# Cross-attention with a state-space tail on one Trainium2 core: the score maxima are turned by VectorE instead of TensorE, grouped in pairs in the context stage, and the last V projection gets another PSUM bank

## The chip, the cores and the metric

The kernel runs on one core of a Trainium2 chip. The metric is the device time of one execution in microseconds (us). Engine names in rows are PE (TensorE, matmuls), PEld (TensorE's weight loads), DVE (VectorE), ACT (ScalarE), POOL (GpSimd) and SPq (the DMA queue of SyncE). PSUM has eight banks of 512 fp32 words per partition; TensorE writes them, VectorE and ScalarE read them.

## The reference, cut to what matters

```python
x = layernorm(builder_state, g1, beta1)            # 4096 x 512
base_n = layernorm(base_state, g1, beta1)          # 3202 x 512, the context
q, k, v = heads(x, Wq, bq), heads(base_n, Wk, bk), heads(base_n, Wv, bv)     # 8 heads of 64
scores = einsum('bhqd,bhkd->bhqk', q, k) / sqrt(64)
out = softmax(scores) @ v ; x = residual + out @ W_o.T + b_o
U = (layernorm(x, g2, beta2) @ W_in.T + b_in) @ Bmat
s = silu(s @ A.T) + u_t                            # a scan over 4096 tokens
result = x + s @ Cmat + program_probs.mean(1) @ W_prog.T + b_prog
```

The change touches only how the softmax obtains, for each query, the number that is subtracted from its scores: their maximum over the keys (taken over scores of reduced precision).

## The kernel before

**Stages.** Token groups of 256 rows are normalised, turned by TensorE (`turn`), and projected: 16 groups `n` of queries, then 13 context groups (`g` = 0 to 12, `n` = 16 + `g`) to keys (`project_k`, four chunks of heads) and values (`project_v`, two tiles). Then comes the attention: 32 units `u`, each of one block of 512 queries and one pair of heads; a unit has 13 steps `j` of two key tiles. Then come the output projection, the second norm, the scan and the output. All engines have their programs written out by hand; semaphores alone tie them. What stands below is in the order of the code.

**Maxima.** Before unit `w` runs, its maxima must be known. For each of 26 numbers `m`, `maxima(w, m)` makes one pair of matmuls (one per head, each on 64 rows of the array): queries of one quarter (`m % 4`) as the stationary operand against 512 keys (`m // 4`); the last two, `m` = 24 and 25, take the 130 keys left over. `take_max(w, m)` on VectorE reduces the pair to a column of `mx_part`. Unit `u` has two of them in every step for the unit after it, so that `m` = 24, 25 of unit `u + 1` stand in step 8 of unit `u`. 34 of them are done early, in the context stage (`ctx_maxima`): in groups 2 to 11 two of unit 0, and from group 3 on most often a third of another; in group 12 the last five.

**From maxima to shift.** `row_max(w)` (L1016) reduces `mx_part` to `mx_row` (128 partitions, 8 columns). `turn_max(w)` (L1364) turns it on TensorE to 8 rows of 128, ScalarE's `shift(w)` (L725) copies it with its sign changed to `shift_row`, and SyncE's `send_shift(w)` writes it to memory and reads it back as `sh[w % 2]`; `spread_shift` also loads it to all partitions as `shb`. Two ways use it: `shift_scores` on TensorE adds `ones_row` times `sh` to the scores of a tile, and for the odd tiles of units after the first VectorE adds `shb` in `add_shift` (L1094). ScalarE then takes the exponential (L799). In step 9 (`TURN_STEP`) of a unit stand `turn_max(u + 1)` on TensorE and `shift(u + 1)` on ScalarE.

**Banks.** In the context stage `turn` writes banks 0 and 1, K chunks use 2 to 4, `project_v` 7, and the early maxima 5 and 6, one pair after another. In the attention scores use banks 0 to 3, maxima 4 and 5, the P times V product 6, and 7 is shared by `turn_max` and the sums over keys (`spread_sum`, step 3).

**GpSimd** adds up exponentials in `accp` (L605) and issues DMAs that add others in `acca` and `accb`; the sum of a unit ends in `acca` (L636) and is read in step 3 of the next.

## Time and profile before

| what | us |
|---|---|
| runs shown | 2253.38, 2254.17, 2255.58; median 2254.17 |
| profiled execution | 2255.61, its span 2253.8 |
| TensorE busy | 2216.3 (98%) |
| VectorE busy | 1713.4 (76%) |
| GpSimd busy | 1584.2 (70%) |
| ScalarE busy | 1092.4 (48%) |

The span runs from the first to the last instruction of the profile; 1.8 us lie around it. The queries' projections end at about 133 us, the context stage at 316 us, the attention at about 2080 us. A row of a timeline gives the start, the duration, engine, line, operation, tiles, shapes and count, and in brackets the idle time of the engine before it with what ended it. A busy PE is one whose pipeline holds a matmul; the distance between the starts of two groups of matmuls says better what a group costs.

### The profile page before, as it was taken

The page shows a single profiled execution, that of the slowest core. Times are in us where ns is not written, and L with a number is a line of the kernel's source. Part 1 is how long each engine was busy: PE and PEld are TensorE (multiplying, and loading weights), DVE is VectorE, ACT ScalarE, POOL GpSimd, SP SyncE. Part 2 cuts the span into 40 slices and gives each one's busy share as a digit, 9 for nine tenths or more (in the row PEclk, how much of TensorE's full clock was granted, in tenths as well). Part 3 has the DMA queues.
Part 4 walks back from the last instruction along what each step waited for, and adds up shares of the span by engine and source line. Part 5 has one row for each costly group of instructions (what it writes and reads, how often), then busy time and mean ns, then how long its engine had stood idle before and what let it go on. Part 6 is the DMA issues. An engine that isn't in the chain of part 4 may idle for free.

```text
span 2253.8 us, 36015 instructions
## 1 busy us (share of the span) xinstructions
PE 2216.3 (98%) x14120; PEld 1279.2 (57%) x14120; DVE 1713.4 (76%) x2087; ACT 1092.4 (48%) x1418; POOL 1584.2 (70%) x1038
## 2 busy tenths in 40 slices
PE   8999999999999999999999999999999999999997
PEld 8998865555555555555555555555555555445774
DVE  7866546888888888888888888888888888763776
ACT  5654334444454444444544544444445444453454
POOL 1200027888888888888888888888888888889332
PEclk9999999999999999999999999999999999999999
DMA  7750226777777777777777777777777777787844
GB/s 273 233 162 10 75 85 139 156 157 160 156 159 160 159 170 168 171 170 167 168 161 160 167 170 171 171 171 164 163 163 165 167 166 166 160 182 159 265 149 150
DMA packets 170091, 365.45 MB, mean 162 GB/s; under 512 B 28537, under 2 KB 75001, under 8 KB 169410
## 3 DMA queue, kind: packets, MB, share of 16 engines
q0 software_dynamic: 59904, 218.13, 47.4%
q1 hardware_dynamic: 110018, 145.02, 20.3%
q8 instruction: 112, 1.84, 0.3%
q14 instruction: 57, 0.47, 0.1%
HBM read 95.82 MB, written 49.04 MB: 64 GB/s over the span
## 4 chain that ended last, share of the span: by engine, by line
PE 94%; DMA 1%; ACT 1%; DVE 1%; issue 1%; POOL 1%; SPq 0%; DVEq 0%; ACTq 0%; POOLq 0%
PE ps L1478 34%; PE ps L1343 11%; PE ps L1455 8%; PE ps L1457 8%; PE ps L1459 8%; PE ps L1447 5%; PE ps L1306 4%; PE ps L1314 3%; PE ps L1324 3%; PE ps L1545 3%; PE ps L1278 1%; DMA acca<-pt 1%; PE ps L1348 1%; PE ps L1488 1%; PE ps L1608 1%
## 5 line engine op out<-in xcount | busy, mean ns | idle before, releaser
L799 ACT ACTIVATE pt<-ps 128x1024 f32<-128x1024 f32 x800 | 777.6, 1021 | 891.8 <-PE ps L1459 882.0
L1005 DVE TENSOR_REDUCE mx_part<-ps 128x2 f32<-128x1024 f32 x768 | 938.1, 1221 | 339.5 <-PE ps L1343 339.5
L605 POOL TENSOR_TENSOR accp<-accp,pt 128x1024 f32<-128x1024 f32 x416 | 1032.9, 2483 | 210.0 <-ACT pt L799 204.7
L1478 PE MATMUL ps<-pt,v 128*64 128x512 f32 x3328 | 805.6, 605 | 0.0
L1094 DVE TENSOR_TENSOR ps<-ps,shb 128x1024 f32<-128x1024 f32 x403 | 493.2, 1224 | 46.7 <-PE ps L1459 46.7
L1478 PEld LDWEIGHTS ps<-pt,v 128*64 128x64 f32 x3328 | 201.8, 136 | 345.2 <-issue 339.0
L1343 PE MATMUL ps<-kk,qh 64*128 64x512 f32 x1520 | 344.4, 448 | 1.6 <-DVE mx_part L1005 1.6
L1343 PEld LDWEIGHTS ps<-kk,qh 64*128 64x128 f32 x1520 | 141.6, 183 | 340.9 <-DVE mx_part L1005 250.0
L1455 PE MATMUL ps<-qh,kk 64*128 64x512 f32 x1664 | 328.9, 390 | 2.7 <-ACT pt L799 2.7
L1457 PE MATMUL ps<-qh,kk 64*128 64x512 f32 x1664 | 329.3, 390 | 0.0
L1459 PE MATMUL ps<-ql,kk 64*128 64x512 f32 x1664 | 328.5, 389 | 0.0
L615 POOL DMA_DIRECT2D acca<-pt x192 | 179.0, 932 | 5.0 <-DMA acca<-pt 3.9
L1455 PEld LDWEIGHTS ps<-qh,kk 64*128 64x128 f32 x1664 | 157.2, 184 | 37.7 <-ACT pt L799 4.1
L1457 PEld LDWEIGHTS ps<-qh,kk 64*128 64x128 f32 x1664 | 157.6, 184 | 34.8
L1459 PEld LDWEIGHTS ps<-ql,kk 64*128 64x128 f32 x1664 | 157.9, 184 | 34.1
L1447 PE MATMUL ps<-sh,ones_row 64*128 64x512 f32 x858 | 173.2, 400 | 1.2 <-ACT pt L799 1.2
L594 POOL MEMSET sh<- 128x512 f32 x2 | 1.0, 530 | 190.3 <-PE ps L1324 190.3
L625 POOL DMA_DIRECT2D accb<-pt x128 | 124.9, 976 | 0.2 <-POOL accp L605 0.2
L1545 PE MATMUL ps<-wo_hl,og 128*128 128x512 f32 x384 | 93.0, 396 | 0.5 <-DVE x_last L1137 0.4
L1447 PEld LDWEIGHTS ps<-sh,ones_row 64*128 64x128 f32 x858 | 82.1, 186 | 15.2 <-ACT pt L799 11.8
L1545 PEld LDWEIGHTS ps<-wo_hl,og 128*128 128x128 f32 x384 | 70.5, 188 | 19.6 <-issue 5.7
L631 POOL TENSOR_TENSOR accp<-accp,accb 128x1024 f32<-128x1024 f32 x32 | 76.9, 2403 | 4.6
(165 smaller groups left out, 1779.7 us busy)
## 6 DMA issues: line engine op xcount, KB each, us to landing
acca<-pt POOLq DMA_DIRECT2D x224, 512.0 KB, 4.9
accb<-pt POOLq DMA_DIRECT2D x160, 512.0 KB, 4.8
q_scratch<-kk SPq DMA_DIRECT2D x32, 512.0 KB, 4.3
acca<-accp POOLq DMA_DIRECT2D x32, 512.0 KB, 4.6
o_scratch<-ost SPq DMA_DIRECT2D x32, 512.0 KB, 3.1
og<-o_scratch SPq DMA_DIRECT2D x32, 512.0 KB, 6.2
shb<-m_scratch SPq DMA_DIRECT2D x31, 512.0 KB, 4.6
xs<-x SPq DMA_DIRECT2D x16, 512.0 KB, 6.5
```

The costliest lines, as they stand in the source:

```text
L605: nc.gpsimd.tensor_tensor(acc[:, :], acc[:, :], pt[n % PT_SLOTS][:, :], ALU.add).then_inc(added_p, 1)
L615: nc.gpsimd.dma_start(acc[:, :], pt[n % PT_SLOTS][:, :], accum_op=ALU.add).then_inc(added_a[u % 2], 16)
L799: nc.scalar.activation(pt[n % PT_SLOTS][:, :], src, ACT.Exp, scale=SCALE).then_inc(exped, 1)
L1005: nc.vector.tensor_reduce(mx_part[w % 2][:, m % QT, :, m // QT], ps[:, b:b + 2, :], AX_X, ALU.max)\
L1094: nc.vector.tensor_tensor(ps[:, b:b + 2, :], ps[:, b:b + 2, :], shb[u % 2][:, :, :], ALU.add)\
L1343: ins = mm(ps[:, bank, :], q[r, (m % QT) * P:(m % QT + 1) * P], kk[r, p, 0, a:a + QB], start=True, stop=True)
L1447: ins = mm(ps[:, 2 * (t % 2) + h, :], ones_row[r, :], sh[u % 2][r, :], start=first, stop=not first)
L1455: mm(ps[:, b + h, :], kk[r, p, 0, key], qh[u % 3][r, :], start=first, stop=False)
L1457: mm(ps[:, b + h, :], kk[r, p, 1, key], qh[u % 3][r, :], start=False, stop=False)
L1459: ins = mm(ps[:, b + h, :], kk[r, p, 0, key], ql[u % 2][r, :], start=False, stop=last)
L1478: ins = mm(ps[HD * h:HD * (h + 1), 6, :], v[:, t, f:f + HD], pt[n % PT_SLOTS][:, h * QB:(h + 1) * QB], start=(t == 0), stop=(t == NT - 1))
L1545: ins = mm(ps[:, 2 + t, :], og[:, d % OG_SLOTS, a, k, rows], wo_hl[:, b, k], start=(i == 0), stop=(i == len(PASSES) - 1))
```

## The change

Four things change together.

1. **Turning.** `turn_max` and `shift` are gone, with their semaphores. `mx_row` is now 32 columns wide (24 of them cleared once), VectorE turns it in blocks of 32 by 32 into `mx_turn`, directly behind the reduction, and `send_shift` stores it with four DMAs of 8 rows by 32 words instead of one of 8 by 128. The sign is no longer changed: `ones_row` holds -1 and `add_shift` subtracts.
2. **Pairing.** In context groups 2 to 11 the second early maximum follows the first directly, ahead of the second V tile, in banks 0 and 1, once those have been read by the norm's copies. VectorE takes it after the second K chunk's low part.
3. **The last V tile** of the context goes to bank 6 (`v_bank`) when all early maxima are taken, so it does not wait for the copy of the tile before it.
4. **`spread_sum`** no longer waits for the shift.

```diff
+def v_bank(n, t):
+    return 6 if n == NG - 1 and t == 1 else 7
+def second_max(g):
+    return (0, 2 * (g - 2) + 1) if 2 <= g < C_G - 1 else None
 def max_bank(w, m):
+    if w == 0 and m % 2 == 1 and m < 2 * (C_G - 3):
+        return 0
     return 5 if (w, m) in EARLY else 4
...
             def send_shift(w):
-                sp.wait_ge(shift_ready, w + 1)
+                sp.wait_ge(max_ready, w + 1)
...
-                sp.dma_start(m_scratch[w % 2].rearrange("h (q k) -> (h q) k", k=P), shift_row[:, :].bitcast(F32)).then_inc(sh_stored, 16)
-                sp.wait_ge(sh_stored, 16 * (w + 1))
+                by_tile = m_scratch[w % 2].rearrange("h (q k) -> (h q) k", k=P)
+                for i in range(4):
+                    sp.dma_start(by_tile[:, 32 * i:32 * (i + 1)], mx_turn[32 * i:32 * i + 2 * QT, :].bitcast(F32)).then_inc(sh_stored, 16)
+                sp.wait_ge(sh_stored, 64 * (w + 1))
...
-            def shift(w):
-                act.wait_ge(max_turned, w + 1)
-                wait(act, sh_stored, 16 * w)
-                nc.scalar.activation(shift_row[:, :], ps[0:2 * QT, turn_bank(w), 0:P], ACT.Copy, scale=-1.0)\
-                    .then_inc(shift_ready, 1)
...
             def row_max(w):
...
-                wait(dve, max_turned, w)
-                nc.vector.tensor_reduce(mx_row[:, :, :].rearrange("p h q -> p q h"), mx_part[w % 2][:, :, :, :], AX_X, ALU.max)\
-                    .then_inc(max_ready, 1)
+                nc.vector.tensor_reduce(mx_row[:, 0:2 * QT].rearrange("p (h q) -> p q h", h=2), mx_part[w % 2][:, :, :, :], AX_X, ALU.max)\
+                    .then_inc(row_ready, 1)
+                dve.wait_ge(row_ready, w + 1)
+                wait(dve, sh_stored, 64 * w)
+                nc.vector.transpose(mx_turn[:, :].bitcast(F32), mx_row[:, :].bitcast(F32)).then_inc(max_ready, 1)
...
             def turn(n):
                 pe.wait_ge(normed, n + 1)
                 wait(pe, n_ready, 2 * n)
+                if second_max(n - 2 - X_G):
+                    pe.wait_ge(max_taken, nth_max(*second_max(n - 2 - X_G)) + 1)
...
             def project_v(n, t):
                 g = n - X_G
-                wait(pe, v_ready, GT * g + t)
+                if v_bank(n, t) == 7:
+                    wait(pe, v_ready, GT * g + t)
+                else:
+                    pe.wait_ge(max_taken, M_EARLY)
...
-                wait(pe, max_taken, nth_max(w, m))
+                if max_bank(w, m) == 0:
+                    wait(pe, max_taken, nth_max(w, m) - 1)
+                    pe.wait_ge(n_ready, 2 * (X_G + m // 2 + 2 + 2))
+                else:
+                    wait(pe, max_taken, nth_max(w, m))
...
             project_v(NG - 1, 0)
-            turn_max(0)
             project_v(NG - 1, 1)
             pe.wait_ge(k_ready, FC * C_G)
-            pe.wait_ge(shift_ready, 1)
+            pe.wait_ge(max_taken, M_EARLY)
...
-                    if ahead and j == TURN_STEP:
-                        turn_max(u + 1)
```

On TensorE, in a context group with three maxima, the order before is this (x11 is the rest of 12 matmuls; `qh` marks a maximum of unit 0, `qx` one of unit 1; L1314 is V, L1324 a K chunk, L1343 a maximum, L1278 the turning of the next group).

```order
L1343 MATMUL ps<-kk,qh_64 128x512 [waits max_taken,k_ready]
L1343 MATMUL ps<-kk,qh_64 128x512
L1314 MATMUL ps<-wkv,n_63 128x512 [waits v_ready]
L1314 MATMUL ps<-wkv,n_63 128x512 x11
L1343 MATMUL ps<-kk,qh_64 128x512 [waits max_taken,k_ready]
L1343 MATMUL ps<-kk,qh_64 128x512
L1324 MATMUL ps<-n_63,wkv 128x256 [waits k_ready]
L1324 MATMUL ps<-n_63,wkv 128x256 x11
L1324 MATMUL ps<-n_63,wkv 128x256 [waits k_ready]
L1324 MATMUL ps<-n_63,wkv 128x256 x11
L1343 MATMUL ps<-kk,qx 128x512 [waits max_taken,k_ready]
L1343 MATMUL ps<-kk,qx 128x512
```

In the changed kernel, where V is L1321, K L1331 and a maximum L1354, the same place reads so.

```order
L1354 MATMUL ps<-kk,qh_64 128x512 [waits max_taken,k_ready]
L1354 MATMUL ps<-kk,qh_64 128x512
L1354 MATMUL ps<-kk,qh_64 128x512 [waits n_ready,max_taken,k_ready]
L1354 MATMUL ps<-kk,qh_64 128x512
L1321 MATMUL ps<-wkv,n_63 128x512 [waits v_ready]
L1321 MATMUL ps<-wkv,n_63 128x512 x11
L1331 MATMUL ps<-n_63,wkv 128x256 [waits k_ready]
L1331 MATMUL ps<-n_63,wkv 128x256 x11
L1331 MATMUL ps<-n_63,wkv 128x256 [waits k_ready]
L1331 MATMUL ps<-n_63,wkv 128x256 x11
L1354 MATMUL ps<-kk,qx 128x512 [waits max_taken,k_ready]
L1354 MATMUL ps<-kk,qx 128x512
```

The second pair of maxima has moved ahead of the V tile and stands beside the first, with one wait more.

In step 9 of a unit of the attention, TensorE has this before, from the end of the scores (L1459) over the second maximum (L1343) to P times V (L1478).

```order
L1455 MATMUL ps<-qh_65,kk 128x512 x2
L1457 MATMUL ps<-qh_65,kk 128x512 x2
L1459 MATMUL ps<-ql_68,kk 128x512 x2
L1364 MATMUL ps<-ident,mx_row 8x128 [waits den_taken,max_ready]
L1343 MATMUL ps<-kk,qh_64 128x512 [waits max_taken]
L1343 MATMUL ps<-kk,qh_64 128x512
L1478 MATMUL ps<-pt_71,v 64x512 [waits exped]
L1478 MATMUL ps<-pt_71,v 64x512
```

And this in the changed kernel.

```order
L1455 MATMUL ps<-qh_65,kk 128x512 x2
L1457 MATMUL ps<-qh_65,kk 128x512 x2
L1459 MATMUL ps<-ql_68,kk 128x512 x2
L1354 MATMUL ps<-kk,qh_64 128x512 [waits max_taken]
L1354 MATMUL ps<-kk,qh_64 128x512
L1478 MATMUL ps<-pt_71,v 64x512 [waits exped]
L1478 MATMUL ps<-pt_71,v 64x512
```

The turning of the row maxima is gone, and the maximum follows the scores, all of them on 64 rows of the array.

At the end of the context stage TensorE has this before, from the last early maxima over the two V tiles to the first maximum of the attention.

```order
L1348 MATMUL ps<-kk,qh_64 128x130 [waits max_taken,k_ready]
L1348 MATMUL ps<-kk,qh_64 128x130 x3
L1314 MATMUL ps<-wkv,n_63 128x512 [waits v_ready]
L1314 MATMUL ps<-wkv,n_63 128x512 x11
L1364 MATMUL ps<-ident,mx_row 8x128 [waits n_ready,max_ready]
L1314 MATMUL ps<-wkv,n_63 128x512 [waits v_ready]
L1314 MATMUL ps<-wkv,n_63 128x512 x11
L1343 MATMUL ps<-kk,qh_65 128x512 [waits max_taken,ones_set,qh_loaded_1,shift_ready,k_ready]
```

And this in the changed kernel.

```order
L1359 MATMUL ps<-kk,qh_64 128x130 [waits max_taken,k_ready]
L1359 MATMUL ps<-kk,qh_64 128x130 x3
L1321 MATMUL ps<-wkv,n_63 128x512 [waits v_ready]
L1321 MATMUL ps<-wkv,n_63 128x512 x11
L1321 MATMUL ps<-wkv,n_63 128x512 [waits max_taken]
L1321 MATMUL ps<-wkv,n_63 128x512 x11
L1354 MATMUL ps<-kk,qh_65 128x512 [waits max_taken,ones_set,qh_loaded_1,k_ready]
```

The turning between the V tiles is gone, and the second V tile waits for maxima taken instead of the copy of the first tile.

## Rows read from the trace of the kernel before

**Rows 1.** The page, part 1: busy us, share of the span, instructions
```profile
PE 2216.3 (98%) x14120; PEld 1279.2 (57%) x14120; DVE 1713.4 (76%) x2087; ACT 1092.4 (48%) x1418; POOL 1584.2 (70%) x1038
```

**Rows 2.** TensorE in steps 7 to 10 of a unit: start, duration (us)
```profile
1005.28 0.50 PE L1343 MATMUL ps<-kk,qh 64*128 64x512 f32 x2
...
1005.62 0.39 PE L1447 MATMUL ps<-sh,ones_row 64*128 64x512 f32 x2
...
1007.23 0.39 PE L1343 MATMUL ps<-kk,qh 64*128 64x512 f32 x2
...
1007.55 1.94 PE L1478 MATMUL ps<-pt,v 128*64 128x512 f32 x8
...
1009.42 0.44 PE L1348 MATMUL ps<-kk,qh 64*128 64x130 f32 x4
...
1013.50 0.50 PE L1343 MATMUL ps<-kk,qh 64*128 64x512 f32 x2
...
1015.53 0.08 PEld L1364 LDWEIGHTS ps<-ident,mx_row 128*8 128x8 f32 x1 [0.35 <-issue]
...
1018.04 0.50 PE L1343 MATMUL ps<-kk,qh 64*128 64x512 f32 x2
```

**Rows 3.** Line L1364: duration ns min/median/max, first and last start us
```profile
L1364 PE MATMUL ps<-ident,mx_row x32: 272/273/274, 311.9 to 2003.1; 128*8 128x128 f32 x32
```

**Rows 4.** Timeline of VectorE and GpSimd at the row maximum (L1016) of that unit
```profile
1012.69 2.37 POOL L605 TENSOR_TENSOR accp<-accp,pt 128x1024 f32<-128x1024 f32 x1 [0.94 <-ACT pt L799]
...
1012.75 0.21 DVE L1016 TENSOR_REDUCE mx_row<-mx_part 128x8 f32<-128x56 f32 x1
...
1014.11 1.23 DVE L1005 TENSOR_REDUCE mx_part<-ps 128x2 f32<-128x1024 f32 x1 [1.15 <-PE ps L1343]
```

**Rows 5.** Timeline of TensorE, a context group without maxima
```profile
146.04 2.99 PE L1314 MATMUL ps<-wkv,kk 128*128 128x512 f32 x12
...
148.87 3.04 PE L1324 MATMUL ps<-kk,wkv 128*128 128x256 f32 x24
```

**Rows 6.** Timeline of TensorE, context group 6
```profile
216.25 3.03 PE L1324 MATMUL ps<-n,wkv 128*128 128x256 f32 x24
219.21 0.49 PE L1343 MATMUL ps<-kk,qh 64*128 64x512 f32 x2
219.64 3.06 PE L1314 MATMUL ps<-wkv,n 128*128 128x512 f32 x12
222.62 0.50 PE L1343 MATMUL ps<-kk,qh 64*128 64x512 f32 x2
223.06 3.12 PE L1324 MATMUL ps<-n,wkv 128*128 128x256 f32 x24
226.11 0.49 PE L1343 MATMUL ps<-kk,qx 64*128 64x512 f32 x2
226.53 1.09 PE L1278 MATMUL ps<-ident,xs 128*128 128x128 f32 x8
```

**Rows 7.** Timeline at the end of the context: PEld, ACT, SPq
```profile
307.45 4.18 PEld L1314 LDWEIGHTS ps<-wkv,n 128*128 128x128 f32 x12
...
311.68 0.08 PEld L1364 LDWEIGHTS ps<-ident,mx_row 128*8 128x8 f32 x1
...
312.39 0.57 ACT L714 ACTIVATE v<-ps 128x512 f32<-128x512 f32 x1
...
312.56 0.30 SPq L413 DMA_DIRECT2D m_scratch<-shift_row  x1
...
313.01 2.61 PEld L1314 LDWEIGHTS ps<-wkv,n 128*128 128x128 f32 x12 [1.25 <-ACT v L714]
...
313.79 0.57 SPq L415 DMA_DIRECT2D sh<-m_scratch  x1
```

**Rows 8.** Windows: busy us by engine (PE, PEld, DVE, ACT, POOL), PEclk, DMA
```profile
307.00:312.00 5.00, 4.92 (x17) 3.73 (x17) 0.92 (x2) 0.00 (x0) 0.00 (x0) 0.66 0.70 243
```

**Rows 9.** Timeline: the latest sum over the keys in the loop
```profile
1923.91 0.16 PEld L1488 LDWEIGHTS ps<-acca,ones 128*32 128x32 f32 x8 [0.89 <-DMA acca<-accp]
```

More of the change, by code:

```diff
@@ L55, in maxima_of @@
     return [(i // NM, i % NM) for i in range(first, min(first + 2, NM * UNITS))]
-TURN_STEP = NJ - M_LEAD
 PAIR_ORDER = [2, 3, 0, 1]
@@ L770, in _ @@
                 high_k(C_G - 1, i)
-            shift(0)
             for t in range(GT):
@@ L825, in _ @@
                         high_o(u - 1)
-                    if j == TURN_STEP and u + 1 < UNITS:
-                        shift(u + 1)
                     if u == UNITS - 2 and j in (3, 5, 7, 9):
@@ L1000, in take_max @@
                 if m == 0:
-                    wait(dve, max_ready, w - 1)
+                    wait(dve, row_ready, w - 1)
                 dve.wait_ge(max_done, nth_max(w, m) + 1)
@@ L1071, in _ @@
                     if g < C_G - 1:
+                        low_k(g, 0)
                         for w, m in early[:1]:
                             take_max(w, m)
-                        for i in (0, 1):
-                            low_k(g, i)
+                        low_k(g, 1)
                         for w, m in early[1:2]:
@@ L1356, in early_maxima @@
                     maxima(w, m)
-            def turn_max(w):
-                pe.wait_ge(max_ready, w + 1)
-                wait(pe, den_taken, w - 1)
-                if w == 0:
-                    pe.wait_ge(n_ready, 2 * NG)
-                nc.tensor.transpose(ps[0:2 * QT, turn_bank(w), 0:P], mx_row[:, :, :].rearrange("p h q -> p (h q)"), ident[:, :])\
-                    .then_inc(max_turned, 1)
             pe.wait_ge(consts, 2)
@@ L1484, in spread_sum @@
                 pe.wait_ge(added_a[u % 2], 16 * (len(A_TILES) + 1) * (u // 2 + 1))
-                if u + 1 < UNITS:
-                    pe.wait_ge(shift_ready, u + 2)
+                wait(pe, den_taken, u)
                 for i in range(4):
```

24 lines of the change are left out of this document (12 added, 12 removed).

## The prediction

> **What bounds the kernel now.** I read the page's shares first, then the timeline of TensorE in the attention, where the kernel spends about 1760 of its 2254 us. TensorE is busy for 2216.3 of 2253.8 us; VectorE, next, has 76% and GpSimd 70% [rows 1]. So what leaves TensorE's queue is time won, as long as no other engine then ends last. In the timeline the reader should compare the distances between the first maxima of successive steps: step 7 takes 1009.42 - 1005.28 = 4.14 us, step 8, whose two maxima are the short ones of 130 keys, takes 4.08, and step 9, which alone holds the turning of the row maxima, takes 1018.04 - 1013.50 = 4.54 [rows 2]. Within a step a pair of 64-row matmuls that follows the first maximum starts 0.34 us after it (1005.62), and the product with V, on all 128 rows, starts 0.32 us behind the second maximum (1007.55 after 1007.23) [rows 2].
>
> **The change part by part.**
>
> Turning in the loop. TensorE loses L1364, one matmul of 0.27 us, 32 in all: 31 in the attention, one at the end of the context [rows 3]. Its price is not the 0.27 but what the step gets longer: the array leaves the 64-row scores (its weight load sat idle for 0.35 us), does the turning, and goes back to 64 rows for the second maximum, which now follows the scores directly. 4.54 - 4.14 = 0.40 us a unit, times 31 = 12.4 us. From below, the idle 0.35 alone gives 10.9; from above, 4.54 - 4.08 gives 14.3 [rows 2]. I take 12.4, since step 7 has the same matmuls as step 9 without its turning.
>
> What VectorE gets in return. It turns 128x32 words, an operation that the trace does not show, and waits for its own reduction before it. The nearest row is that reduction of 56 elements a partition, 0.21 us; the farthest, the reduction of 1024, takes 1.23 [rows 4]. 32 elements are nearer to the first: I take 0.2, with 0.1 for the wait. Queued behind it is the first maximum of step 9, and for that VectorE stands idle for 1.15 us, until TensorE has made it [rows 4]. So the turning is hidden, and costs nothing; at 1.23 plus the wait it would run over by 0.2 us, and this much VectorE would be late in step 9. The Trainium skill ("VectorE: DVE Perf Modes", section The three transpose paths) gives 311 ns for VectorE's turning of 128x128 bf16. An estimate by that page, about 0.3 us here, would leave the sum as it is; no run so far shows it.
>
> ScalarE loses 32 small copies; it is busy for 48% [rows 1] and nothing hangs on it. SyncE issues four stores of the shift instead of one, some 4 x 0.3 us by L413 [rows 7], but starts when VectorE is done in step 8, over 4 us ahead of the old start behind step 9. The loads `sh` and `shb` queued behind them come earlier, not later, and are first needed in step 0 of the next unit.
>
> Pairing in the context. In group 6 from the first maximum to the turning of the next group is 226.53 - 219.21 = 7.32 us: pair to V 0.43, V to pair 2.98, pair to K 0.44, K to pair 3.05, pair to turning 0.42 [rows 6]. Afterwards the order is pair, pair, V, K, K, pair: 0.34 for the first pair and 0.32 for the second, as steps of the loop show them [rows 2], V to K 2.83 as in a group without maxima [rows 5], K to pair 2.96 as it is behind an undisturbed V (216.25 to 219.21), and 0.42: 6.87 us. This saves 0.45 us in each of ten groups, 4.5 us. From below, with 0.43 instead of 0.32 and 3.05 instead of 2.96, it is 0.25, 2.5 us; from above, if the second pair takes no more than its 512 columns at 2.4 GHz, 0.21 instead of 0.32, it is 0.56, 5.6 us. The new waits cost nothing by the rows: between the turning that fills banks 0 and 1 and the pair that wants them stand a V tile and two K chunks, 2.83 + 2.96 = 5.8 us, as many as between the pair and the next turning, and VectorE has two reductions of 1.23 and a few smaller operations to do in each. The first pair uses banks 5 and 6, the second 0 and 1, so neither waits for the reduction of the other.
>
> End of the context. V's first tile loads its last weights until 307.45 + 4.18 = 311.63; then TensorE turns the row maxima at 311.68, ScalarE copies the shift and then the tile until 312.96, and the second tile starts at 313.01 [rows 7]. With its own bank, and all early maxima taken long before, it can start at about 311.65: 1.35 us. TensorE's clock belongs to this place: over 307 to 312 the granted clock is 0.66 on the mean [rows 8], which is 3.4 us at 1.2 instead of 2.4 GHz. If the lower level lasted into the second tile, twelve matmuls that load weights for 2.61 us could lose up to 2.6; at the other bound the clock is back as before. I take 1.35, from -1.2 to 1.4. The shift of unit 0 must then arrive earlier. It is ready on VectorE 3 us before the old copy, its four stores take some 1.2 us to issue, and the store's way to the next issue is 313.79 - 312.56 = 1.23 us [rows 7]; `sh` would be issued at about 311.5, 2.3 us sooner than now, where only 1.35 are asked for. Covered.
>
> Sum: 12.4 + 4.5 + 1.35 = 18.2 us. The profiled execution took 2255.61 with a span of 2253.8; it becomes 2235.6 in span and 2237.4 in time. It lies 1.4 above the median of the runs, 2254.17, which becomes 2236.0. By the lower bounds the sum is 10.9 + 2.5 - 1.2 = 12.2 (2242.0), by the upper ones 14.3 + 5.6 + 1.4 = 21.3 (2232.9).
>
> **The rivals.**
>
> *The sums over the keys become late* (chance 0.08). Each unit of the attention becomes 0.4 us shorter for GpSimd and its DMAs too. `spread_sum` in step 3 waits for the last DMA into `acca`, and in one unit TensorE's weight load stood for 0.89 us because of it [rows 9]. If GpSimd could not follow at all, the 12.4 us would be given back, and the time would be 2254.17 - 5.8 = 2248.3. For it speaks that one unit; against it GpSimd's 70% and that in the unit of rows 4 it sat idle for 0.94 us ahead of one addition, waiting for ScalarE.
>
> *Pairing gives nothing* (0.11). The two pairs wait for something between them, a bank or VectorE, or the V tile starts later by what the pair gained. Then 4.5 us are missing: 2240.5. Against it speaks that VectorE has 2.98 us between the two pairs now, and two reductions of 1.23 with a K chunk's low part between fit before the second K chunks are done.
>
> *Slower: VectorE's turning is held up by GpSimd* (0.05). In the unit read, GpSimd begins an addition at 1012.69 that lasts 2.37 us, to 1015.06, and VectorE would come to its turning at about 1013.0, behind its reduction [rows 4]. If the turning could not run beside it, VectorE would be free at about 1015.3 and its first maximum of step 9 start 1.2 us late. Each step hangs from VectorE's second maximum of the step before with hardly 0.1 us to spare (the first reduction begins 0.61 us into the step, and it, the addition of the shift, on as many elements, and the second reduction take about 1.2 us each, an estimate of 4.1 of the 4.14 us), so all 1.2 us would reach TensorE, 31 x 1.2 = 37 us: 2236 + 37 = 2273. It decides from 18.2 / 31 = 0.6 us of overrun in a unit on, that is from 1.75 us of turning with its waits. Against it: the reduction at 1012.75 ran in 0.21 us beside the same addition. The Trainium skill ("SBUF — State Buffer", section Who interferes with whom) says that VectorE's copies and `tensor_scalar` can enter modes that use a port pair shared with GpSimd, where the second to come is blocked for a whole instruction, and that reductions never do; of the turning it says nothing. The reduction's row agrees with the page. The page's rule, if it held for the turning, would be this rival.
>
> **How the numbers follow.** The forecast that the sum holds gets the remaining 0.76. A measurement of this kernel can tell about 0.2%, 4.5 us, from no change. The time predicted is the forecast's, 2236. Its own bounds, 2232.9 to 2242.0, hold the second rival's 2240.5 too; with the run-to-run scatter of about 1 us this gives 2232 to 2243, which leaves out the first and the third rival, 0.13, and a little of the tails. Faster by over 0.2%: the forecast, the second rival and most of the first, 0.93; within 0.2%: 0.02; slower: 0.05.
>
> **What would show it.** In the profile after: step 9 of a unit takes 4.14 us, and units follow each other 0.4 us closer; the turning on VectorE takes 0.1 to 0.3 us and the idle time before its next maximum is shorter by as much and still above 0; a context group with three maxima takes 0.45 us less; the second V tile of the last group starts within 0.1 us of the first one's last weights. The prediction is wrong if steps 8 or 9 get longer on VectorE, if `spread_sum` waits for `acca` in many units, or if the clock falls in places where it stood at its upper level before.

## The result, and the profile after

The changed kernel takes 2241.92 us (median of five runs, 2239.28 to 2242.49), the kernel before 2254.17 (five runs). The ratio is 0.9941, with a 95% interval of 0.9928 to 0.9954: faster by 12.25 us, and by the interval 10.4 to 16.2, where the sum said 18.2. The profiled execution took 2239.28 us with a span of 2237.5, so the two profiled executions lie 16.3 us apart. The missing 6 us thus have two parts: 1.9 us that the profiled pair lacks of the sum, and 4.1 us by which the medians lie closer together than the profiled pair (the profiled execution of before lies 1.4 above its median, that of after 2.6 below its own). The second part is hardly more than the interval of the ratio allows.

The page of the changed kernel, part 1, answers to [rows 1]: TensorE lost 15.9 us of busy time and 32 instructions, VectorE gained 5.1 us and 33 instructions.

```profile
PE 2200.4 (98%) x14088; PEld 1275.1 (57%) x14088; DVE 1718.5 (77%) x2120; ACT 1088.5 (49%) x1386; POOL 1586.4 (71%) x1038
```

The timeline of TensorE in step 9 and the step behind it (a maximum is now L1354), to be read against [rows 2]:

```profile
786.89 0.50 PE L1354 MATMUL ps<-kk,qh 64*128 64x512 f32 x2
...
788.61 0.39 PE L1459 MATMUL ps<-ql,kk 64*128 64x512 f32 x2
788.83 0.44 PE L1354 MATMUL ps<-kk,qh 64*128 64x512 f32 x2
789.20 1.94 PE L1478 MATMUL ps<-pt,v 128*64 128x512 f32 x8
791.07 0.50 PE L1354 MATMUL ps<-kk,qh 64*128 64x512 f32 x2
...
795.21 0.50 PE L1354 MATMUL ps<-kk,qh 64*128 64x512 f32 x2
```

The second maximum follows the scores after 0.22 us. Step 9 takes 791.07 - 786.89 = 4.18 us, the next 4.14. Over the 30 units between the first and the last short maxima of the attention, step 9 is 4.19 on the mean where it was 4.56: 0.37 a unit, not 0.40. The missing 0.04 is between the second maximum and the product with V (0.37 us in step 9, 0.32 in [rows 2]). The units as a whole follow each other 0.42 us closer (54.89 to 54.47). Half of what goes beyond step 9 is one pause: TensorE of the kernel before waits 1.09 us at 1926.30, behind the place of [rows 9], for ScalarE, which waits for a DMA into `acca`; the changed kernel has 0.30 us there. The weight load of [rows 9] itself says little: it sits idle for 0.81 us in the 30 other units too, and in 30 units of the changed kernel.

VectorE at the row maximum, against [rows 4]:

```profile
1003.90 0.21 DVE L1014 TENSOR_REDUCE mx_row<-mx_part 128x8 fp32r<-128x56 f32 x1
1004.15 0.21 DVE L1018 STREAM_TRANSPOSE mx_turn<-mx_row 128x32 f32<-128x32 f32 x1
1005.25 1.23 DVE L1002 TENSOR_REDUCE mx_part<-ps 128x2 f32<-128x1024 f32 x1 [0.89 <-PE ps L1354]
```

The turning takes 0.21 us, starts 0.25 us behind the start of the reduction, and leaves 0.89 us of idle time ahead of the next maximum. It took 0.21 us all 32 times, and 31 of the 32 lay wholly inside an addition of GpSimd.

TensorE in context group 6, against [rows 6]:

```profile
215.89 3.03 PE L1331 MATMUL ps<-n,wkv 128*128 128x256 f32 x24
218.85 0.73 PE L1354 MATMUL ps<-kk,qh 64*128 64x512 f32 x4
219.51 3.06 PE L1321 MATMUL ps<-wkv,n 128*128 128x512 f32 x12
222.41 3.03 PE L1331 MATMUL ps<-n,wkv 128*128 128x256 f32 x24
225.37 0.49 PE L1354 MATMUL ps<-kk,qx 64*128 64x512 f32 x2
225.79 0.87 PE L1282 MATMUL ps<-ident,xs 128*128 128x128 f32 x6
```

Both pairs are one group of four, 0.66 us long, and nothing in it waits. From the first maximum to the next turning is 6.94 us where it was 7.32: 0.38 instead of the 0.45 of the sum, because V to K takes 2.90 and not 2.83.

The end of the context, the first maximum of the attention before, then TensorE and SyncE's queue of the changed kernel, against [rows 7]:

```profile
315.97 0.50 PE L1343 MATMUL ps<-kk,qh 64*128 64x512 f32 x2
```

```profile
304.49 0.44 PE L1359 MATMUL ps<-kk,qh 64*128 64x130 f32 x4 [1.08 <-DVE mx_part L1006]
304.86 7.36 PE L1321 MATMUL ps<-wkv,n 128*128 128x512 f32 x24
312.15 0.50 PE L1354 MATMUL ps<-kk,qh 64*128 64x512 f32 x2
```

```profile
306.31 1.31 SPq L419 DMA_DIRECT2D m_scratch<-mx_turn  x4
309.94 0.57 SPq L421 DMA_DIRECT2D sh<-m_scratch  x1
```

The two V tiles are one group now. The first maximum of the attention starts at 312.15, 3.82 us earlier than before (315.97), the first V tile 2.59 us earlier: the place itself gave 1.23. `sh` is issued 2.2 us ahead of the attention's first maximum and 3.85 us earlier than before, of which 2.59 are the earlier stage; the 1.26 that are left are less than the prediction's 2.3, but TensorE has no wait for `sh` at the start of the attention.

**Where the profiled pair lost 1.9 us of the sum.** I followed the same marks through both traces. At the last maximum (L1359, for unit 31) the changed kernel is 16.4 us ahead, where the sum, with 30 of its 31 steps 9, has 17.9. Of this 1.4 us, 0.7 are the pairing's, 0.1 the end of the context's, and 1.1 lie ahead of the first early maximum, which starts at 165.07 us instead of 163.95; the loop gave 0.6 more than its term. At the first output projection the lead is 15.0; at the end 16.3. What comes back at the end goes with the clock: in the output stages the granted clock is 0.53, 0.50, 0.50 and 0.76 over 2226 to 2234 us before, and 0.97, 0.50 and 0.68 over 2208 to 2214 after, which is 3.4 and 1.7 us of the upper level's time. The stretch that gives time back is the last unit, 1.4 us, or 1.8 with the 31st turning that it has no more. There TensorE, ScalarE and GpSimd wait for DMAs. The rows are of the changed kernel, for SyncE, GpSimd, ScalarE and TensorE in this order:

```profile
1999.79 2.61 SPq L499 DMA_DIRECT2D og<-o_scratch  x4
...
2011.54 0.89 POOL L642 DMA_DIRECT2D acca<-accp  x1 [3.89 <-DMA acca<-pt]
...
2019.45 1.02 ACT L798 ACTIVATE pt<-ps 128x1024 f32<-128x1024 f32 x1 [3.64 <-DMA acca<-pt]
...
2020.53 0.50 PE L1455 MATMUL ps<-qh,kk 64*128 64x512 f32 x2 [2.67 <-ACT pt L798]
```

And of the kernel before, GpSimd, ScalarE and TensorE at the same place of the program:

```profile
2028.39 0.89 POOL L636 DMA_DIRECT2D acca<-accp  x1 [4.03 <-DMA acca<-pt]
...
2034.48 1.02 ACT L799 ACTIVATE pt<-ps 128x1024 f32<-128x1024 f32 x1 [1.80 <-DMA acca<-pt]
...
2035.56 0.50 PE L1455 MATMUL ps<-qh,kk 64*128 64x512 f32 x2 [1.08 <-ACT pt L799]
```

SyncE loads the attention's outputs for the first projection (`og`, 2 MB in four DMAs) while the last accumulating DMAs of unit 30 are under way. The accumulating DMA beside them takes 9.6 us to land before and 9.8 after, and GpSimd's next one is issued after a wait of 4.03 and 3.89 us. TensorE's wait at 2035.56 (before) and 2020.53 (after) grew from 1.08 to 2.67 us. From the last maximum to the first projection is 74.7 us before and 76.1 after.

**The longer wait comes from a later DMA.** The activation that TensorE waits for at 2020.53 waits for the accumulating DMA issued at 2013.10, when all four loads of `og` have landed (the last at 2012.3). This DMA takes 6.2 us. The profile's view of the DMAs has it, and while it is under way, from 2015.9 to 2016.5 us, a packet of another queue:

```profile
acca<-pt POOLq DMA_DIRECT2D x1, 512.0 KB, 6.2
...
q8 instruction: 1, 0.02, 9.3%
```

The second line is a packet of 16 KB of the queue that the profile calls instruction. The same DMA in `step9_same`, which is the changed kernel with one matmul more in step 9 (below), and TensorE behind it:

```profile
acca<-pt POOLq DMA_DIRECT2D x1, 512.0 KB, 4.4
...
2021.51 0.50 PE L1455 MATMUL ps<-qh,kk 64*128 64x512 f32 x2 [1.09 <-ACT pt L798]
```

Eleven profiles of this case have the loads of `og` at their old place. In five of them (the changed kernel, `after_again`, `turn_only`, `dve_4`, `dve_8`) such a packet starts 33.1 to 33.6 us behind the last maximum, while this DMA is under way; the DMA takes 6.10 to 6.25 us, TensorE waits 2.66 to 2.76, and the stretch takes 76.1 to 78.8. In the other six (before, `pair_only`, `bank_only` and the three of `step9`) the packet comes outside of it; the DMA takes 4.4 us, TensorE waits 1.08 to 1.10, and the stretch takes 74.1 to 75.0. The five have no matmul at the place of the turning in step 9, the six have one. So the longer wait goes with the change, but by where the packet falls, and not because the last unit stops what TensorE won upstream: `step9_same` has the turning on VectorE and takes 74.8. That the packet delays the DMA is an inference from this coincidence; no run moved the packet alone.

### The profile page after: what moved, and what is told of

The parts are those of the page before. It is cut to its first block, busy times and chain, and to the rows that moved or that the text cites. A ratio compares the mean times of both kernels' runs of the same rounds, so it can differ in the third digit from the quotient of the medians.

```text
span 2237.5 us, 35987 instructions
## 1 busy us (share of the span) xinstructions
PE 2200.4 (98%) x14088; PEld 1275.1 (57%) x14088; DVE 1718.5 (77%) x2120; ACT 1088.5 (49%) x1386; POOL 1586.4 (71%) x1038
## 4 chain that ended last, share of the span: by engine, by line
PE 93%; DMA 2%; issue 1%; ACT 1%; POOL 1%; DVE 1%; SPq 0%; DVEq 0%; ACTq 0%; POOLq 0%
PE ps L1478 33%; PE ps L1354 11%; PE ps L1455 8%; PE ps L1457 8%; PE ps L1459 8%; PE ps L1447 4%; PE ps L1310 4%; PE ps L1542 4%; PE ps L1321 3%; PE ps L1331 3%; DMA acca<-pt 1%; PE ps L1282 1%; POOL accp L611 1%; PE ps L1359 1%; PE ps L1487 1%
## 5 line engine op out<-in xcount | busy, mean ns | idle before, releaser
L611 POOL TENSOR_TENSOR accp<-accp,pt 128x1024 f32<-128x1024 f32 x416 | 1044.1, 2510 | 193.1 <-ACT pt L798 191.8
L1478 PE MATMUL ps<-pt,v 128*64 128x512 f32 x3328 | 805.6, 605 | 0.0
L1478 PEld LDWEIGHTS ps<-pt,v 128*64 128x64 f32 x3328 | 201.8, 136 | 344.6 <-issue 338.2
L1354 PE MATMUL ps<-kk,qh 64*128 64x512 f32 x1520 | 339.2, 444 | 1.7 <-DVE mx_part L1002 1.6
L1354 PEld LDWEIGHTS ps<-kk,qh 64*128 64x128 f32 x1520 | 140.9, 183 | 340.5 <-DVE mx_part L1002 257.7
L1459 PE MATMUL ps<-ql,kk 64*128 64x512 f32 x1664 | 328.1, 389 | 0.0
L621 POOL DMA_DIRECT2D acca<-pt x192 | 189.6, 987 | 5.4 <-DMA acca<-pt 4.0
L1459 PEld LDWEIGHTS ps<-ql,kk 64*128 64x128 f32 x1664 | 157.3, 184 | 34.4
L1447 PEld LDWEIGHTS ps<-sh,ones_row 64*128 64x128 f32 x858 | 82.1, 186 | 15.0 <-ACT pt L798 12.4
```

Source lines behind the costliest of these rows:

```text
L611: nc.gpsimd.tensor_tensor(acc[:, :], acc[:, :], pt[n % PT_SLOTS][:, :], ALU.add).then_inc(added_p, 1)
L621: nc.gpsimd.dma_start(acc[:, :], pt[n % PT_SLOTS][:, :], accum_op=ALU.add).then_inc(added_a[u % 2], 16)
L1354: ins = mm(ps[:, bank, :], q[r, (m % QT) * P:(m % QT + 1) * P], kk[r, p, 0, a:a + QB], start=True, stop=True)
L1447: ins = mm(ps[:, 2 * (t % 2) + h, :], ones_row[r, :], sh[u % 2][r, :], start=first, stop=not first)
L1459: ins = mm(ps[:, b + h, :], kk[r, p, 0, key], ql[u % 2][r, :], start=False, stop=last)
L1478: ins = mm(ps[HD * h:HD * (h + 1), 6, :], v[:, t, f:f + HD], pt[n % PT_SLOTS][:, h * QB:(h + 1) * QB], start=(t == 0), stop=(t == NT - 1))
```

## The experiments

What was open: whether each part of the change is worth what its rows say, where the rest of the 18.2 us went, and whether the price of 0.40 us for a matmul of 8 columns is that of the array's shape. Medians of "before" are those of the runs timed beside them on the same chip.

### The parts alone

`turn_only` is the changed kernel without pairing and without the bank; `pair_only` and `bank_only` are the kernel before with one part each; `after_again` is the changed kernel once more, timed beside them.

```diff
 # turn_only, on the changed kernel
-    return 6 if n == NG - 1 and t == 1 else 7
+    return 7
...
-    return (0, 2 * (g - 2) + 1) if 2 <= g < C_G - 1 else None
+    return None
...
-                        early_maxima(early[:2])
+                        early_maxima(early[:1])
                         project_v(n, 1)
+                        early_maxima(early[1:2])
...
 # pair_only, on the kernel before: the same lines the other way round, with max_bank's
+    if w == 0 and m % 2 == 1 and m < 2 * (C_G - 3):
+        return 0
...
 # bank_only, on the kernel before
-                wait(pe, v_ready, GT * g + t)
+                if v_bank(n, t) == 7:
+                    wait(pe, v_ready, GT * g + t)
+                else:
+                    pe.wait_ge(max_taken, M_EARLY)
...
```

> The kernel before with the first part of the change alone: the row maxima are turned by VectorE, and stored by four DMAs; early maxima and V banks as before. Theory A (the gain is the sum of what TensorE's queue loses, as the timelines show it): the units follow each other 0.39 us closer, 31 x 0.39 = 12.1 us, and the second V tile of the last context group still waits for ScalarE's copy, so about 12 to 12.5 us in all, ratio 0.9946. Theory B (the whole change gained 12.3 to 13.3 us in timed runs where its own timeline shows 16.3 because something in the loop gives time back that no single profile shows): well below 12 us, 8 or so.

> The kernel before with the second part alone: in context groups 2 to 11 the second early maximum stands beside the first, in banks 0 and 1. Theory A: ten groups of 13.58 instead of 13.96 us, 3.8 us, ratio 0.9983. Theory B (the pairing's gain is given back elsewhere, for example in a lower granted clock at the end of the context): about 1 us or nothing.

> The kernel before with the third part alone: the last V tile goes to bank 6 and does not wait for ScalarE's copy of the tile before it; the turning on TensorE still stands between the two. Theory A: the tile starts at about 312.0 instead of 313.0, 1.0 us. Theory B: the time at the lower clock gets longer by what was won, no gain.

> The changed kernel once more, so that it and its parts are timed on the same chip against the same runs of before. Theory A: the gain is the sum of the three parts run beside it, 16 us or so by the timelines. Theory B: less than the sum, 12 to 13 us as measured before.

| kernel | us (runs' lowest to highest) | ratio, 95% interval | below before (2253.63) |
|---|---|---|---|
| turn_only | 2244.12 (2243.26 to 2247.25) | 0.9961 (0.9947 to 0.9974) | 9.5 |
| pair_only | 2250.11 (2247.88 to 2253.69) | 0.9984 (0.9975 to 0.9993) | 3.5 |
| bank_only | 2251.75 (2250.10 to 2255.31) | 0.9995 (0.9986 to 1.0004) | 1.9 |
| after_again | 2241.68 (2241.37 to 2242.66) | 0.9948 (0.9934 to 0.9961) | 12.0 |

The order of the parts is that of the sum. Turning and pairing show by themselves; the bank's 1.9 us can't be told from nothing. The profiles give each part more sharply. In `turn_only` units follow each other 0.39 us closer, as expected, 11.7 us over 30 units. In `pair_only` the way from the first early maximum to the attention is 3.8 us shorter, as expected (148.26 instead of 152.02). In `bank_only` the two V tiles with the turning take 1.1 us less (7.39 instead of 8.52). The three medians add up to 14.9 us where all together give 12.0; an interval of a single ratio is some 3 us to each side for the short series, so this difference is not established.

The profile of `after_again` tells something that the first profile didn't: the clock. The rows are windows of 2 us in the last unit (span of the window, busy time of PE, PEld, DVE, ACT, POOL, granted clock, DMA share, GB/s), of the changed kernel's first profile and then of `after_again`:

```profile
2018.00:2020.00 2.00, 0.00 (x0) 0.00 (x0) 0.00 (x0) 0.55 (x1) 1.33 (x2) 1.00 0.40 162
2020.00:2022.00 2.00, 1.47 (x12) 1.05 (x12) 0.46 (x1) 0.48 (x1) 2.00 (x2) 1.00 0.35 68
```

```profile
2018.00:2020.00 2.00, 0.01 (x2) 0.00 (x0) 0.00 (x0) 0.40 (x1) 1.39 (x1) 0.90 0.48 193
2020.00:2022.00 2.00, 1.32 (x6) 1.13 (x8) 0.00 (x0) 0.62 (x1) 1.96 (x2) 0.50 0.34 68
2022.00:2024.00 2.00, 2.00 (x10) 0.97 (x10) 1.56 (x2) 0.35 (x1) 2.00 (x2) 0.50 1.03 197
2024.00:2026.00 2.00, 2.00 (x6) 0.47 (x4) 0.00 (x0) 1.86 (x3) 1.44 (x2) 0.50 0.69 131
2026.00:2028.00 2.00, 2.00 (x14) 1.01 (x12) 0.00 (x0) 0.00 (x0) 1.93 (x2) 0.89 0.74 132
```

In both TensorE stands still for the whole of 2018 to 2020. In the first profile the granted clock stays 1.00; in the second it falls to 0.50, the 1.2 GHz level, while the engine stands and stays there until 2026. The five windows lose 0.2 + 1 + 1 + 1 + 0.2 = 3.4 us of the upper level's time, and from the last maximum to the first projection takes 78.8 us instead of 76.1. `turn_only` shows the same (0.79, 0.50 and 0.86 from 2024 to 2030; 77.5 us), and so do `dve_4` (0.60 and 0.55 from 2020 to 2024; 77.4 us) and `dve_8` (0.74, 0.50 and 0.91 from 2048 to 2054; 77.4 us): 1.7 us each. The six profiles whose wait there is 1.1 us stay at 1.00. The mean clock of a run fits this: 3.4 us are 0.0015 of the span, and the first five runs of the changed kernel are 2239.28 and 2239.89 us at a mean clock of 0.998, and 2241.92, 2242.24 and 2242.49 at 0.996. That the slower three are the ones with this fall isn't shown. A mean over a whole run does not say where the clock fell, and it falls in two more places that differ between profiles: at the end of the context by 0 or 1.7 us of the upper level's time, in the output stages by 0, 1.7 or 3.4. Two of the runs of `after_again` took 2241.4 us at 0.998.

### The loads of the last unit moved

The loads of `og` are issued behind `spread_rden(u - 1)` of the last unit instead of ahead of it, when the accumulating DMAs have landed: `og_late_before` on the kernel before, `og_late_after` on the changed one.

```diff
                     sp.wait_ge(shifted, tiles_added(UNITS - 1))
-                    for d in (0, 1):
-                        load_og(d)
...
                     spread_rden(u - 1)
+                if u == UNITS - 1:
+                    for d in (0, 1):
+                        load_og(d)
```

> The kernel before, with the first four loads of the output projection's operand (og, 2 MB) issued behind the inverse sums of unit 30 instead of at the start of the last unit. Theory A (those loads collide with the last DMAs into acca of unit 30, whose landing then takes about 10 instead of 5 us, and ScalarE and TensorE wait): the last unit gets 2 to 4 us shorter, ratio 0.9985. Theory B (GpSimd's additions bound the last unit anyway, and the loads only happen beside): no change, or slower if the loads are then missed by the projection.

> The changed kernel with the same later loads. Theory A (the change wins 16 us up to the last unit, and loses 1.4 to 4 of them where these loads stand, by a longer pause of TensorE and the lower clock behind it): the pause of 2.7 us goes, the granted clock stays at its upper level there, and the kernel gains 4 to 6 us on the changed one; against the kernel before with late loads it is 15 to 16 us faster. Theory B (the missing 4 us of the timed runs are lost elsewhere): as much as the kernel before gains from late loads, so 12 to 13 us apart again.

In the traces the collision is gone from both: the accumulating DMA that took 9.6 and 9.8 us to land takes 5.1 and 4.9, the last maximum to the first projection takes 71.9 us (before: 74.7) and 72.1 us (after: 76.1), and in `og_late_after` TensorE has no pause at all in the stretch where it stood for 2.67 us. So the collision is shown to cost 2.8 us there in the kernel before, as theory A said; it is older than the change. The changed kernel's 4.0 us are not the collision's alone, since the later DMA takes 5.0 us in `og_late_after` instead of 6.2. In `og_late_alt` (below), whose loads are late too, it takes 6.5 us with an instruction packet beside it, TensorE waits 1.30 us at that place, and the stretch takes 73.6.

Late loads also cost something: in the first output projections TensorE now waits 2.19 us (`og_late_before`), 0.89 (`og_late_after`) and 2.00 (`og_late_alt`) for VectorE's `x_first`, where no profile with early loads has more than 0.41. Of the lead of 3.4 us that `og_late_after` has over the changed kernel at the first projection, 2.6 are left at the last one and 1.5 at the end (span 2236.0 against 2237.5), where its granted clock also lost 3.4 instead of 1.7 us.

In the timed runs the kernel before goes from 2254.55 to 2252.63 us (0.9992, 0.9983 to 1.0001), which can't be told from nothing, and the changed one stands at 2240.29 (0.9937, 0.9923 to 0.9950), 1.4 to 1.6 us below the earlier runs of the changed kernel. With late loads the two medians are 12.3 us apart, as theory B said and not 15 to 16. So it is not shown that the 4 us missing in the timed runs are lost at these loads; the intervals are too wide to exclude it.

`og_late_alt` adds to `og_late_after` that the odd early maxima of the last context group use banks 0 and 1 as well, so that TensorE doesn't wait for VectorE there.

```diff
-    if w == 0 and m % 2 == 1 and m < 2 * (C_G - 3):
+    if w == 0 and m % 2 == 1:
         return 0
...
-                    pe.wait_ge(n_ready, 2 * (X_G + m // 2 + 2 + 2))
+                    pe.wait_ge(n_ready, 2 * min(X_G + m // 2 + 2 + 2, NG))
```

> The changed kernel with late loads and, in the last context group too, odd early maxima of unit 0 in banks 0 and 1, so that none of the five waits for the reduction of the one before. Theory A (the pauses of 0.25, 0.25 and 1.1 us there go, and with the last one the 3.4 us at the lower clock behind it): 1.6 us from the pauses and up to 1.7 more from the clock, about 3 us faster than the kernel with late loads alone. Theory B (the clock falls there whatever these pauses are): 1 to 1.5 us.

It takes 2236.59 us (2233.24 to 2239.80), a ratio of 0.9915 (0.9902 to 0.9929) to the kernel before: the fastest median here, 17.96 us below before. It is 3.7 us below `og_late_after`, but the two intervals overlap (0.9923 to 0.9950), so the times alone don't choose between the theories. The end of its context stage, TensorE, and then the same of `dve_4`, whose context stage is the changed kernel's:

```profile
302.67 0.67 PE L1360 MATMUL ps<-kk,qh 64*128 64x130 f32 x8 [0.26 <-DVE mx_part L1003]
303.26 5.74 PE L1322 MATMUL ps<-wkv,n 128*128 128x512 f32 x24
308.93 0.50 PE L1355 MATMUL ps<-kk,qh 64*128 64x512 f32 x2
```

```profile
304.44 0.44 PE L1361 MATMUL ps<-kk,qh 64*128 64x130 f32 x4 [1.08 <-DVE mx_part L1006]
304.81 5.74 PE L1323 MATMUL ps<-wkv,n 128*128 128x512 f32 x24
310.47 0.50 PE L1356 MATMUL ps<-kk,qh 64*128 64x512 f32 x2
```

The pause of 1.08 us is gone: the last two groups of maxima are one. The pause of 0.26 ahead of them, and the one of 0.25 before it, are still there, so the expectation's list of what goes was too long. The two V tiles take 308.93 - 303.26 = 5.67 us instead of the changed kernel's 312.15 - 304.86 = 7.29. In the windows from 304 to 310 the granted clock is 1.00, where the changed kernel had 0.81, 0.50 and 0.84. But the clock is not shown to be the edit's doing: `dve_4` has the pause of 1.08 us, keeps 1.00 in the same windows, and takes 310.47 - 304.81 = 5.66; so does `step9_half`, with 5.65. Of the 13 profiles with this pause the clock stayed up in four (`dve_4`, `step9_half`, `turn_only`, `og_late_before`) and fell in nine. Against `dve_4`, at the same clock, the way from the first early maximum to the attention is 1.3 us shorter (144.14 against 145.44), which is theory B's size. The rest of the 3.7 us of the timed runs is not accounted for.

### What a matmul of another shape costs

Step 9 gets a matmul back whose result nobody reads, in the place where the turning stood. Each run has one of the three lines below; the flags `start` and `stop` are left out.

```diff
                         score_tile(u, 2 * j + 1)
+                    if ahead and j == 9:
+                        wait(pe, den_taken, u)
+                        mm(ps[0:8, 7, 0:P], ones[:, 0:8], ident[:, :])                   # step9_full
+                        mm(ps[0:8, 7, 0:P], ones[0:HD, 0:8], ident[0:HD, :])             # step9_half
+                        mm(ps[:, 7, 0:P], ones_row[0:HD, :], sh[u % 2][0:HD, 0:P])       # step9_same
                     for w, m in todo[1:]:
```

> The changed kernel with one matmul of constants put back where the turning stood in step 9 of every unit (128 rows, 8 columns of weights, 128 moving columns; its result is not used). Theory A (the price of the turning was that the array leaves the 64-row matmuls and comes back): step 9 takes 4.54 us again, 0.40 more. Theory B (the price was the turning's own waits for VectorE): 4.14 to 4.25 us.

> The same matmul on 64 rows only (its result is not used), so that it stands among 64-row matmuls. Theory A: what is left is its own 128 columns and issue, 0.05 to 0.1 us; step 9 takes about 4.2 us. If the price is the matmul's and not that of leaving the 64 rows: 4.5 us.

> The changed kernel with one matmul more in step 9 of each of 31 units, of 128 columns into bank 7, on 64 rows with 128 weight columns and fp32r operands: the array shape and type of the scores and maxima around it. It has 31 matmuls whose result is not read; the output does not depend on it. The 8-column matmuls cost 0.53 us a unit (4.67 and 4.66 us for step 9 instead of 4.14). Theory A2 (the price is that of a change of the array's shape, there and back): here nothing changes shape, so step 9 takes 4.14 + 0.05 to 0.15 = 4.2 to 4.3 us, and the one run lies 2 to 5 us above the changed kernel, 2241 to 2247. Theory B (any extra matmul with weights of its own between the scores and the second maximum costs about that much): step 9 takes 4.6 to 4.7 us, and the run 2250 to 2254.

TensorE in step 9 of one unit, from the added matmul or the scores ahead of it to the second maximum, first of `step9_full` (128 rows, 8 columns of weights), then of `step9_half` (64 rows, 8 columns), then of `step9_same` (64 rows, 128 columns, as all its neighbours):

```profile
791.96 0.39 PE L1459 MATMUL ps<-ql,kk 64*128 64x512 f32 x2
792.28 0.39 PE L1523 MATMUL ps<-ident,ones 128*8 128x128 f32 x2
792.60 0.50 PE L1354 MATMUL ps<-kk,qh 64*128 64x512 f32 x2
```

```profile
791.00 0.38 PE L1523 MATMUL ps<-ident,ones 64*8 64x128 f32 x2
791.31 0.50 PE L1354 MATMUL ps<-kk,qh 64*128 64x512 f32 x2
```

```profile
788.37 0.39 PE L1459 MATMUL ps<-ql,kk 64*128 64x512 f32 x2
788.60 0.22 PE L1523 MATMUL ps<-sh,ones_row 64*128 64x128 f32 x1
788.61 0.49 PE L1354 MATMUL ps<-kk,qh 64*128 64x512 f32 x2
```

Over 30 units step 9 takes 4.66, 4.66 and 4.26 us, against 4.19 without the matmul: the price is 0.47, 0.47 and 0.07. The runs give 2251.72, 2249.74 and 2240.68 us, one each. In the first two the small matmul starts 0.32 us behind the last scores, where scores follow each other after 0.23, and the next group 0.31 us behind it; in the third it starts 0.23 behind the last scores and the maximum at once behind it. `step9_same` fell where its expectation had the price of a change; the expectation for `step9_half` was wrong: leaving the rows of the array as they are doesn't avoid the price. So it is shown that the price isn't that of one more matmul, but of one that differs from its neighbours. All three wait for the same semaphore, so it isn't that wait either. The number of matmuls isn't it: the first two are two in the rows, the turning of the kernel before was one and cost 0.37.

In what it must differ, these three runs don't show: the first two, like the turning of the kernel before, have plain fp32 operands on 8 columns, the third has its neighbours' type (fp32r) and shape, so type and shape changed together. The ordinary step doesn't separate them either. A group of the same shape follows the scores after 0.22 or 0.23 us (788.61 to 788.83 in the changed kernel), the product with V after 0.32, and the second 64-row pair behind it starts 0.34 us after the first [rows 2]; but `v` and `pt` are plain fp32 and the scores are fp32r. The pairing separates them. In a context group the maxima (64 rows), the V tiles and the K chunks (128 rows) are all fp32r, and putting two pairs of maxima side by side takes away one change of shape and one change back, with the same matmuls (the second pair in other banks). That is worth 7.32 - 6.94 = 0.38 us, the size of the turning's 0.37. So a change of shape there and back costs about as much as the turning did with the type left alone; what a change of type costs alone wasn't tried.

### How much room VectorE has

`dve_4` and `dve_8` let VectorE turn the same block four and eight times more ahead of the one that counts.

```diff
                 wait(dve, sh_stored, 64 * w)
+                for _ in range(4):                 # dve_8: range(8)
+                    link(nc.vector.transpose(mx_turn[:, :].bitcast(F32), mx_row[:, :].bitcast(F32)))
                 nc.vector.transpose(mx_turn[:, :].bitcast(F32), mx_row[:, :].bitcast(F32)).then_inc(max_ready, 1)
```

> The changed kernel with four more turnings of the same row on VectorE before the one that counts, each waiting for the one before (about 0.25 us each, 1.0 in all). VectorE stands idle for 0.7 to 0.9 us before its next maximum now. Theory A (what goes beyond that idle time reaches TensorE): steps 9 get up to 0.2 us longer, 31 x 0.2 = 6 us at most. Theory B (VectorE has more room behind): no change.

> The same with eight more, about 2.0 us. Theory A: 1.1 to 1.2 us longer in each of 31 units, 35 us, the size of the rival in which GpSimd holds up the turning. Theory B: much less, since TensorE has other work in front of it.

`dve_4` takes 2239.90 us, no more than the changed kernel, and its step 9 is 4.19 us on the mean, as there: theory B. Its VectorE goes from the turning to the next maximum without any idle time and is still on time:

```profile
786.20 0.21 DVE L1020 STREAM_TRANSPOSE mx_turn<-mx_row 128x32 f32<-128x32 f32 x1
786.33 1.21 DVE L1002 TENSOR_REDUCE mx_part<-ps 128x2 f32<-128x1024 f32 x1
```

`dve_8` takes 2269.50 us. VectorE and then TensorE in its step 9:

```profile
793.53 1.94 DVE L1019 STREAM_TRANSPOSE mx_turn<-mx_row 128x32 f32<-128x32 f32 x8
795.51 0.21 DVE L1020 STREAM_TRANSPOSE mx_turn<-mx_row 128x32 f32<-128x32 f32 x1
795.64 1.18 DVE L1002 TENSOR_REDUCE mx_part<-ps 128x2 f32<-128x1024 f32 x1
```

```profile
796.88 0.49 PE L1356 MATMUL ps<-kk,qh 64*128 64x512 f32 x2 [0.73 <-DVE mx_part L1002]
```

VectorE is held for 795.51 - 793.53 = 1.98 us more. Its reduction starts 2.11 us behind the first turning, in the changed kernel 1.10 (1005.25 - 1004.15): 1.01 us late. TensorE's second maximum waits 0.73 us for it. Step 9 becomes 5.14 us on the mean, 0.95 more; 31 times that is 29 us, and the run is 28 to 30 us above the changed kernel's; the expectation had 35. Nearly all of VectorE's overrun reaches TensorE (0.95 of 1.01 us), as the slower rival said, and it begins between the 1 us of four further turnings and the 2 us of eight.

## Why the prediction was right, and where its sum was off

**The bound.** TensorE was and is the bound; its loss of work became time. Right.

**Turning in the loop.** 0.40 us a unit was taken from step 9 against step 7 [rows 2]. Measured are 0.37 in step 9 and 0.42 in a whole unit, between the two profiles; 12.4 us was the term, 12.6 is what the stretch of 30 units got shorter, of which step 9 gave 11. Putting a matmul of 8 columns back cost 0.47. That the price isn't that of the matmul's own work is shown (0.07 us for a larger one of the neighbours' kind). "Leaves the 64-row scores" was too narrow a name for it, since 64 rows with 8 columns in plain fp32 cost the same; that a change of shape alone has this price, the pairing shows (0.38 us).

**VectorE's turning.** 0.2 us plus 0.1 of wait was the estimate; 0.21 and 0.04 it was. Hidden under the idle time as said, with 0.7 to 0.9 us of it left. The Trainium skill ("VectorE: DVE Perf Modes", section The three transpose paths) gives 311 ns for another size and type, and the estimate from it was 0.3; the trace has 0.21 for 128x32 fp32, and the turning is hidden by either.

**Pairing.** 0.45 a group was the term, 0.38 it gave, 3.8 us for ten groups; `pair_only` gives 3.5. The mis-sized piece is V to K: a V tile that stands behind maxima takes 2.90 us, where the row of a group without maxima [rows 5] had 2.83.

**End of the context.** 1.35 predicted, 1.23 measured. The clock was lower there both before and after, by 1.7 us of the upper level's time in each, so it moved little between the two. Profiles of either kernel in which it stayed at 1.00 have 6.93 us (`og_late_before`) and 5.66 (`dve_4`) for the V tiles, 1.27 apart. `sh` came 1.26 us sooner against the V tiles and not 2.3; it was still in time.

**Where the sum was off.** In the profiled pair it is off by 1.9 us. The term that was mis-sized is pairing (4.5, measured 3.8). The other pieces are no terms of the sum: 1.1 us ahead of the first early maximum, which starts anywhere from 163.9 to 165.5 us in the 14 profiles, 1.8 in the last unit, and 1.3 us back in the output stages, where the clock fell for less time. The prediction took the last unit to pass TensorE's savings on, and it does (74.8 us in `step9_same`, 74.7 before); what costs time there is a wait of 2.67 us for a late DMA beside a packet of the instruction queue, and behind it, in four of the five profiles that have this wait, 1.7 or 3.4 us of the upper level's time. This is one of the prediction's own signs of being wrong, a fall of the clock where it stood at its upper level before, and it came; the sum has no term for it.

The other 4.1 us, between the profiled pair and the medians, stay open. Scatter of the clock in three places can make such a difference, but no run shows that it is it, and the experiment that would have found it in the last unit's loads gave theory B's distance. The measured 2241.92 lies near the upper end of the range, 5.9 us above the forecast of 2236. The range holds it because the lower bounds of all terms were added up; that they covered a shortfall of another origin is luck.

**The rivals.** Pairing gives nothing: refuted, 0.38 us a group and `pair_only`'s interval below 1. Sums late in every unit: refuted, units are 0.42 us closer. Its row was misread: the weight load of [rows 9] sits idle for 0.81 us in the other units too, and the pause that tells is the 1.09 us behind it. VectorE held up by GpSimd: did not come, 0.21 us in all 32 turnings, 31 of them inside an addition of GpSimd; its chain from VectorE to TensorE is real and its price nearly right (0.95 us of step for 1.01 of lateness), but the turning is nowhere near the point where it decides. The Trainium skill's rule on the shared port ("SBUF — State Buffer", section Who interferes with whom) would hold up the later of the two for a whole instruction if it applied to this turning; by these rows it doesn't.

## What to carry to other kernels

Price a small matmul by the step with and without it, not by its duration: one of 8 columns in plain fp32 among groups of another shape and type cost 0.37 to 0.47 us, one of the neighbours' shape and type 0.07. Put matmuls of the same shape side by side: that alone gave 0.38 us a group. When a stage gets longer, follow the wait back to the one DMA or instruction that ended it, and look in every profile that is there whether the same wait is as long: here five profiles of eleven had it, and one matmul more in step 9, whose result nobody reads, took it away. A pause of the bounding engine may cost more than its length, if the granted clock falls behind it: behind the one in the last unit 3.4 us of the upper level's time were lost in one profile, 1.7 in three, nothing in the fifth. And before a clock that stayed up is put down to an edit, look whether it stayed up without the edit too.

## What the runs showed of the hardware that was not expected

The same pause of TensorE in the same place (2018 to 2020 us, nothing issued) left the granted clock at 1.00 in one execution and brought it to 0.50 for over 6 us in another of the same kernel. A DMA of 512 KB that accumulates into SBUF, 4.9 us from issue to landing in the median, took 9.6 and 9.8 us when four loads of 512 KB from another queue were issued beside it, and GpSimd waited 4.03 and 3.89 us for it; with the loads issued later it took 5.1 and 4.9. And the same DMA of a later tile took 4.4 us in six profiles, and 6.10 to 6.25 in the five in which a packet of 16 KB of the instruction queue came beside it; one matmul more in step 9 of every unit went with the packet coming earlier.
